# Reordering the first batch: value product square by square, keys tile by tile, the third context later

## The chip, the cores and the metric

The kernel runs on one core of a Trainium2 chip. The metric is the device time of one execution in microseconds (us), median of several runs. A core has TensorE (PE, matrix products), VectorE (DVE), ScalarE (ACT), GpSimd (POOL) and a queue of transfers that SyncE (SP) issues. Each works through its own list of instructions in order and waits on semaphores for the others.

## The reference, cut to what matters

Sixteen batches of `x`, each 512 rows by 512 columns in float32, pass through two layers:

```
x = x + xattn(layernorm(x), ctx, lens)
x = x + ffn(layernorm(x))

xattn:  h = rmsnorm(embeds) @ W_in.T + b_in
        u = rmsnorm(ctx)[..., :512] * gain          # input of a scan
        s = scan over the rows of ctx:  s[i] = a * s[i-1] + u[i]
        out = s[plug(row)] + h                      # rows of s picked by index
ffn:    xr = mu_r*y + (1-mu_r)*y_previous_row       # xk likewise
        r = sigmoid(xr @ W_r.T)
        k = square(relu(xk @ W_k.T))
        out = r * (k @ W_v.T)
```

`a` is so small that four shifted additions (by 8, 4, 2, 1 rows) of the first 128 rows give the scan. With these inputs no batch picks a row of `s` beyond the first 128, so the branches called `far` do nothing.

## The kernel before

A float32 product is made of three matmuls on a high part and a low part: high by high, high by low, low by high. `product` (L561 to L563) issues them. ACT makes the high part by a copy, DVE the low part by a subtraction (`low`, L1003). Every [512 x 512] product is 4 output tiles by 4 terms by 3 matmuls of 128x512, 48 in all. A batch has four such products and one turn by 16 transposes (`turn`, L697).

The work is a pipeline over batches, and its order is written out by hand for each engine, in an `iteration(b)` of each. While batch b is in the feed-forward layer, `nxt = b+1` is in the projection and its layer norm, and `new = b+2` is loaded and scanned. The stretch in question is `iteration(0)`: b is batch 0, nxt batch 1, new batch 2. Batches 0 and 1 have orders of their own (`is_first`), since the weights are still being split there.

On TensorE, iteration 0 runs `gate_product(0)`, `first_key_product(0)`, the value products of the four row tiles, and `turn(1)`. Iteration 1 follows with `project(2)`, `gate_product(1)`, `key_product(1)` and so on. What each waits for:

- `first_key_product` goes over pairs of output tiles (0, 1) and (2, 3), and within a pair over the four terms c. When a tile m is complete, `k_done` lets ACT make square m (`squares`: relu, square, high part), and then DVE its low part (`ka_low`, written to `xr_lo`).
- `value_product(b, t, first, last)` adds the terms m of row tile t, and at t = 0 waits for the low part of each square m.
- `turn(1)` needs `norm_b(1)` of DVE (L1211). That waits for a reciprocal root of POOL, `root_b` (L473).
- `project(2)` needs both halves of `x_lo(2)` of DVE (the low part of the turned x), which follow `x_hi(2)` of ACT.
- `gate_product(1)` needs the low parts of the mixed rows one by one. DVE's `mixing(1, ...)` makes these, at the head of its iteration 1: combine (L1136), high part on ACT, low part on DVE. Its tile 0 takes the terms c = 0 to 3 as they come.

The scan of batch 2 is spread over DVE's list. `squares_c` (ACT) sums the squares of the context, `stats_c` (DVE) scales the sum, `root_c` (POOL, L478) takes the root, `scan_input` (DVE, L1060) makes `u`. Then come four steps. Before each `scan_step`, SP shifts the last result down by two transfers into `above` (`shift_scan`, L366 and L367); they are issued when the step before is done. `add_bias` ends the scan, SP stores it, and POOL adds the picked rows to x by indirect transfers.

POOL's order in an iteration is `root_c(new)`, `root_b(nxt)`, `root_a(new)`, `add_patches(new)`. SP's is load x and turned x of `new`, the shifts and the store of the scan, then the four stores of b. `far_over` frees the context buffer for the next load.

Of the kernel before, what the change touches and what calls it, by code (L numbers as in the profile page):

```python
# [48 lines left out]
def reached(eng, semaphore, batch, per_batch, done):  # L49

    value = batch.number() * per_batch + done
    if isinstance(value, int) and value <= 0:
        return
    eng.wait_ge(semaphore, value)
# [35 lines left out]
def build(nc, x, x_turned, ctx, patch_lens, w_in, b_in, columns, g_init, w_r, w_k, w_v, out):  # L90

    B, S, D = x.shape
    DG = ctx.shape[2]
    C = D // P
    T = S // P
# [11 lines left out]
    with ExitStack() as stack:  # L107
# [135 lines left out]
        def tile(t):  # L243
            return slice(t * P, (t + 1) * P)

        def is_first(b, n=0):
            return b.fixed and b.number() == n
# [11 lines left out]
        def is_last(b):  # L259
            return b.fixed and b.number() == LAST  # L260
# [297 lines left out]
        def _(pe):  # L558
            def product(where, lhs_hi, lhs_lo, rhs_hi, rhs_lo, start, stop):

                nc.tensor.matmul(where, lhs_hi, rhs_hi, start=start, stop=False)  # L561
                nc.tensor.matmul(where, lhs_hi, rhs_lo, start=False, stop=False)  # L562
                return nc.tensor.matmul(where, lhs_lo, rhs_hi, start=False, stop=stop)  # L563
# [25 lines left out]
            def far(b):  # L589

                n = far_count(pe, b)
                with pe.If(n > 0):
                    earlier = far_earlier(pe, b)
                    for c in range(1, T):
                        done = earlier * (T - 1) + c
                        if c > 1:
                            pe.wait_ge(far_copied, done - 1)
                        else:
                            if b.fixed and b.number() < 2:
                                reached(pe, s_copied, b, 1, 1)  # L600
                            pe.wait_ge(far_u_lo, earlier * T + 1)

                        product(scan_bank(b)[:, :], decay_hi[:, 1, :], decay_lo[:, 1, :], u_hi[:, :], u_lo[:, :],
                                True, False).then_inc(far_carried, 1)
                        pe.wait_ge(far_u_lo, earlier * T + c + 1)
                        product(scan_bank(b)[:, :], decay_hi[:, 0, :], decay_lo[:, 0, :], u_hi[:, :], u_lo[:, :],
                                False, True).then_inc(far_s, 1)

                    pe.wait_ge(far_copied, earlier * (T - 1) + T - 1)
                    hold(pe, pe_passed)  # L610
# [22 lines left out]
            def first_key_product(b):  # L633


                for pair in ((0, 1), (2, 3)):
                    for c in range(C):
                        pe.wait_ge(w_lo_ready[WK], c + 1)
                        reached(pe, mix_lo_ready, b, 2 * C, C + c + 1)
                        for m in pair:  # L640
                            if c == 0:
                                reached(pe, x2_ready, b.plus(1), T, m + 1)
                            last = product(bank[m][:, :], wt_hi[WK][:, c, tile(m)], wt_lo[WK][:, c, tile(m)],
                                           xk_hi[:, c, :], xk_lo[:, c, :], c == 0, c == C - 1)
                            if c == C - 1:
                                last.then_inc(k_done, 1)

            def key_product(b):

# [51 lines left out]
            def iteration(b):  # L701
                nxt, new = b.plus(1), b.plus(2)
                if is_first(nxt):
                    first_steps(new)
                    return
                if nxt.exists(B) and not is_first(nxt, 1):
                    project(nxt)
                if b.exists(B) and not is_last(b):
                    gate_product(b)
                    key_product(b)  # L710
                    if is_last(nxt):
                        turn(nxt)

                    value_product(b, 0, 0, C - 1)
                    value_product(b, 1, 0, C - 1)
                    value_product(b, 0, C - 1, C)
                    value_product(b, 1, C - 1, C)
                if is_last(b):
                    key_product(b)
                    gate_product(b)  # L720
                    for t in range(T - 1):
                        value_product(b, t, 0, C)
                    value_halves(b, T - 1)
                if new.exists(B):
                    far(new)
                if b.exists(B) and not is_last(b):
                    for t in range(2, T):
                        value_product(b, t, 0, C)
                if nxt.exists(B) and not is_last(nxt):
                    turn(nxt)  # L730
# [80 lines left out]
        def _(act):  # L811
# [34 lines left out]
            def squares_c(b):  # L846
                reached(act, ctx_loaded, b, 16, 16)
                reached(act, v_c_done, b.plus(-1), 1, 1)
                nc.scalar.activation(ctx_squared[:, :], ctx_of(b)[:, :], ACT.Square, accum_out=v_c[:, 0:1]).then_inc(ms_c_done, 1)
# [74 lines left out]
            def iteration(b):  # L924
                nxt, new = b.plus(1), b.plus(2)
                if b.exists(B):
                    if is_last(b):
                        mix_hi(b, C, 2 * C)
                        squares(b)
                        gates(b)  # L930
                    elif is_first(b):
                        mix_hi(b, 0, C)
                        weight_hi(WK)
                        mix_hi(b, C, C + 2)
                        gates(b)
                        mix_hi(b, C + 2, C + 3)
                        weight_hi(WV, 0, 2)
                        mix_hi(b, C + 3, 2 * C)
                        squares_c(new)
                        weight_hi(WV, 2, C)  # L940
                    else:
                        mix_hi(b, 0, 2 * C)
                        if new.exists(B):
                            squares_c(new)
                        gates(b)
                if is_first(b):
                    squares(b)
                if is_first(b, 1):
                    squares(b)
                if new.exists(B) and not is_first(new, 1):  # L950
                    x_hi(new, 0)
                    x_hi(new, 1)
                if b.exists(B) and not is_last(b) and not is_first(b) and not is_first(b, 1):
                    squares(b)
                if is_last(nxt):
                    turned_out(nxt)
                    mix_hi(nxt, 0, C)
                if is_first(nxt):
                    x_hi(new, 1)

                    reached(act, far_over, nxt, 1, 1)
                    squares_c(new)
                    weight_hi(WR, 0, 1)
                    turned_out(nxt)
                if nxt.exists(B) and not is_last(nxt) and not is_first(nxt):
                    turned_out(nxt)
# [23 lines left out]
        def _(dve):  # L990
# [244 lines left out]
            def iteration(b):  # L1235
# [55 lines left out]
                if is_first(b):  # L1291
                    add_x(nxt, 2)
                    add_x(nxt, 3)
                    stats_c(new)
                    weight_lo(WV, 2, C)
                    scan_input(new)
                    ka_low(b, 0)
                    clear_head(new)
                    statistics_b(nxt, 0)
                    statistics_b(nxt, 1)  # L1300
                    ka_low(b, 1)
                    stats_b(nxt, 2)
                    scan_step(new, 0)
                    ka_low(b, 2)
                    ka_low(b, 3)
                    norm_b(nxt)
                    scan_step(new, 1)
                    stats_a(new)
                    scan_step(new, 2)
                    gating(b, 0)  # L1310
                    gating(b, 1)
                    x_lo(new, 0)
                    x_lo(new, 1)
                    scan_step(new, 3)
                    add_bias(new)
                    far(new)
                    dve.sem_inc(far_over, 1)
                    add_out(b, 0)
                    add_out(b, 1)
                    gating(b, 2)  # L1320
                    gating(b, 3)
                    add_out(b, 2)
                    add_out(b, 3)
                    return
                if nxt.exists(B):
                    add_x(nxt, 0)
# [191 lines left out]
```

## Time and profile before

| what | value |
|---|---|
| median of 3 runs | 763.27 us (761.37 to 763.87) |
| the profiled execution, its time | 761.57 us |
| its span | 760.0 us |
| PE busy | 745.4 us (98%) |
| DVE busy | 586.7 us (77%) |
| ACT busy | 405.5 us (53%) |
| POOL busy | 171.7 us (23%) |
| mean granted clock of TensorE | 0.991 |

The profile is of one execution, and all times in it count from the start of its span. A row of the timeline is: start, duration, engine, line, operation, output <- inputs, shape, number of instructions merged, and in brackets the idle time ahead of it with what ended it. A PE busy for 98% of the span leaves some 15 us in which it waited, nearly all of it in the first 80 us.

### The profile page before, as it was taken

How to read it: one execution, taken by the hardware profiler on the slowest of the kernel's cores; microseconds unless marked ns; L12 is line 12 of the kernel's file. 1: busy time of each engine (PE TensorE's matmuls, PEld its weight loads, DVE VectorE, ACT ScalarE, POOL GpSimd, SP SyncE). 2: the span in 40 equal slices, each digit the busy share in tenths (PEclk: the TensorE clock that was granted, in tenths of full speed). 3: DMA queues.
4: the chain of work that ended last, by engine and by line, in shares of the span. 5: the costliest groups of instructions: out<-in, count | busy, mean ns of one | idle time of the engine just before them, and what ended most of it. 6: DMA issues, size and time to landing. Idle time of an engine off the chain costs nothing.

```text
span 760.0 us, 11067 instructions
## 1 busy us (share of the span) xinstructions
PE 745.4 (98%) x3432; PEld 616.0 (81%) x3433; DVE 586.7 (77%) x1063; ACT 405.5 (53%) x666; POOL 171.7 (23%) x163
## 2 busy tenths in 40 slices
PE   7988999999999999999999999999999999999998
PEld 5866788888888888888888888888888888888887
DVE  7888996887869778696876879778696977867462
ACT  4177354754545556453754545465364655544860
POOL 6441230313131031312113131121312113130000
PEclk9999999999999999999999999999999999999999
DMA  8667371726446272633716355281634627240011
GB/s 308 172 194 187 117 200 56 206 98 154 138 112 180 69 185 104 159 135 93 205 54 162 129 137 166 79 222 56 153 125 109 193 67 192 96 125 14 1 56 56
DMA packets 51453, 100.02 MB, mean 132 GB/s; under 512 B 5134, under 2 KB 5390, under 8 KB 51388
## 3 DMA queue, kind: packets, MB, share of 16 engines
q1 hardware_dynamic: 41900, 82.46, 31.6%
q0 software_dynamic: 9216, 16.78, 13.4%
q8 instruction: 14, 0.23, 0.1%
q14 instruction: 35, 0.29, 0.1%
q10 hardware_dynamic: 288, 0.27, 0.1%
HBM read 64.26 MB, written 21.76 MB: 113 GB/s over the span
## 4 chain that ended last, share of the span: by engine, by line
PE 92%; DMA 4%; POOL 1%; DVE 1%; issue 1%; ACT 0%; SPq 0%; DVEq 0%; POOLq 0%
PE bank L561 29%; PE bank L562 29%; PE bank L563 29%; PE bank L697 3%; POOL ring L505 1%; DMA ring<-s_rows,patch_now 1%; DMA xt<-in_L_ffn_W_r 1%; PE bank L791 1%; DMA ring<-s_rows,patch_of 1%; DMA above<-u 1%; DMA s_rows<-scanned 1%; PE bank L770 0%; DMA ctx_rows<-in_ctx 0%; DMA lens<-in_mask_BxS_if 0%; POOL rs_a L459 0%
## 5 line engine op out<-in xcount | busy, mean ns | idle before, releaser
L505 POOL DMA_INDIRECT ring<-s_rows,patch_now x60 | 99.9, 1665 | 228.8 <-DMA s_rows<-scanned 198.1
L1136 DVE SCALAR_TENSOR_TENSOR scratch<-turned,cols,scratch 128x512 f32<-128x512 f32 x128 | 94.4, 748 | 32.0 <-ACT scratch L862 21.9
L1003 DVE TENSOR_TENSOR xr_lo<-scratch,xr_hi 128x512 fp32r<-128x512 f32 x124 | 85.1, 688 | 39.8 <-ACT xr_hi L813 38.9
L813 ACT ACTIVATE turned<-bank 128x512 f32<-128x512 f32 x64 | 33.1, 604 | 131.1 <-PE bank L697 131.1
L561 PE MATMUL bank<-wi_hi,xt_hi 128*128 128x512 f32 x256 | 101.9, 398 | 0.0
L561 PE MATMUL bank<-xk_hi,wk_hi 128*128 128x512 f32 x256 | 100.0, 391 | 1.0 <-DVE xk_lo L1003 0.6
L563 PE MATMUL bank<-wi_hi,xt_lo 128*128 128x512 f32 x256 | 100.6, 393 | 0.0
L562 PE MATMUL bank<-wi_lo,xt_hi 128*128 128x512 f32 x256 | 100.5, 393 | 0.0
L561 PE MATMUL bank<-wr_hi,xr_hi 128*128 128x512 f32 x256 | 100.1, 391 | 0.0
L562 PE MATMUL bank<-wr_lo,xr_hi 128*128 128x512 f32 x256 | 100.0, 391 | 0.0
L563 PE MATMUL bank<-wr_hi,xr_lo 128*128 128x512 f32 x256 | 99.8, 390 | 0.0
L563 PE MATMUL bank<-xk_hi,wk_lo 128*128 128x512 f32 x256 | 99.6, 389 | 0.0
L562 PE MATMUL bank<-xk_lo,wk_hi 128*128 128x512 f32 x256 | 99.6, 389 | 0.0
L561 PE MATMUL bank<-wv_hi,xr_hi 128*128 128x512 f32 x240 | 94.4, 394 | 2.6 <-DVE xr_lo L1003 2.6
L562 PE MATMUL bank<-wv_lo,xr_hi 128*128 128x512 f32 x240 | 94.0, 392 | 0.0
L563 PE MATMUL bank<-wv_hi,xr_lo 128*128 128x512 f32 x240 | 93.9, 391 | 0.0
L862 ACT ACTIVATE scratch<-turned,cols 128x512 f32<-128x512 f32 x128 | 89.5, 710 | 0.5
L813 ACT ACTIVATE xr_hi<-scratch 128x512 fp32r<-128x512 f32 x124 | 77.9, 628 | 21.1 <-DVE scratch L1136 19.1
L1217 DVE TENSOR_TENSOR gate<-bank,gate 128x512 f32<-128x512 f32 x63 | 42.6, 689 | 54.2 <-PE bank L563 54.2
L898 ACT ACTIVATE gate<-bank 128x512 f32<-128x512 f32 x64 | 37.2, 593 | 68.9 <-PE bank L563 68.8
L813 ACT ACTIVATE xk_hi<-scratch 128x512 fp32r<-128x512 f32 x64 | 40.5, 632 | 45.5 <-DVE scratch L1136 44.8
L909 ACT ACTIVATE scratch<-bank 128x512 f32<-128x512 f32 x64 | 38.2, 597 | 41.1 <-PE bank L563 37.7
(148 smaller groups left out, 1267.1 us busy)
## 6 DMA issues: line engine op xcount, KB each, us to landing
ring<-in_x SPq DMA_DIRECT2D x16, 1024.0 KB, 5.2
out<-gate SPq DMA_DIRECT2D x63, 256.0 KB, 2.1
xt<-in_x_turned SPq DMA_DIRECT2D x14, 1024.0 KB, 7.2
above<-scanned SPq DMA_DIRECT2D x42, 224.0 KB, 2.7
ctx_rows<-in_ctx SPq DMA_DIRECT2D x15, 512.0 KB, 5.9
s_rows<-scanned SPq DMA_DIRECT2D x15, 256.0 KB, 2.5
above<-u SPq DMA_DIRECT2D x14, 224.0 KB, 2.7
gate<-in_L_xattn_W_in SPq DMA_DIRECT2D x4, 256.0 KB, 3.5
```

The costliest lines, as they stand in the source:

```text
L505: pool.indirect_dma_start(ring[b.slot][:, t, :], None, s_rows[:, :], bass.IndirectOffsetOnAxis(ap=rows, axis=0), compute_op=ALU.add).then_ ...
L561: nc.tensor.matmul(where, lhs_hi, rhs_hi, start=start, stop=False)
L562: nc.tensor.matmul(where, lhs_hi, rhs_lo, start=False, stop=False)
L563: return nc.tensor.matmul(where, lhs_lo, rhs_hi, start=False, stop=stop)
L697: last = nc.tensor.transpose(first_bank(b, t)[:, tile(c)], normed[:, t, c * P:(c + 1) * P], ident[:, :])
L813: return nc.scalar.activation(to, of, ACT.Copy)
L862: nc.scalar.activation(scratch[:, i % 2, :], turned[:, c, 0:S], ACT.Copy, scale=cols[:, 3 + which, c:c + 1]).then_inc(carried, 1)
L898: nc.scalar.activation(gate[:, t, :], bank[4 + t][:, :], ACT.Sigmoid).then_inc(gate_ready, 1)
L909: nc.scalar.activation(scratch[:, m % 2, :], bank[m][:, :], ACT.Relu).then_inc(relu_ready, 1)
L1003: return nc.vector.tensor_tensor(to, whole, high, ALU.subtract)
L1136: nc.vector.scalar_tensor_tensor(scratch[:, 2 + i % 2, :], turned[:, c, 1:S + 1], cols[:, 1 + which, c:c + 1], scratch[:, i % 2, :], ALU.m ...
L1217: nc.vector.tensor_tensor(gate[:, t, :], bank[4 + t][:, :], gate[:, t, :], ALU.mult).then_inc(gated, 1)
```

## The change

There are four edits, all in the first batches' own orders.

1. TensorE, keys: tiles 0 and 1 stay interleaved; tiles 2 and 3 now come one after the other, so tile 2 is complete 12 matmuls before tile 3.
2. TensorE, values: for batch 0, the four row tiles take term 0, then all take term 1, and so on, where before tiles 0 and 1 took terms 0 to 2, then term 3, and tiles 2 and 3 followed whole.
3. ACT: `squares_c(2)` moves from ahead of the squares of batch 0 (and of the last two weight copies) to behind them.
4. DVE: `stats_c(2)` and `scan_input(2)` move behind the low parts of all four squares, and `scan_input` behind `norm_b(1)` too; the statistics of batch 1 come earlier; `x_lo(2)` comes after scan step 0 and no longer after step 2; `far(2)` and the release of the context buffer go to the end.

A wait of `far` on TensorE for the last `gated` is added inside a branch that is not entered here.

```diff
@@ TensorE, far
+                            if is_first(b, 2):
+                                reached(pe, gated, Batch(0, 0), T, T)
@@ TensorE, first_key_product
-                for pair in ((0, 1), (2, 3)):
-                    for c in range(C):
+                order = [(m, c) for c in range(C) for m in (0, 1)] + [(m, c) for m in (2, 3) for c in range(C)]
+                for m, c in order:
+                    if m == 0:
                         pe.wait_ge(w_lo_ready[WK], c + 1)
                         reached(pe, mix_lo_ready, b, 2 * C, C + c + 1)
-                        for m in pair:
...
@@ TensorE, iteration
+                    if is_first(b):
+                        for m in range(C):
+                            for t in range(T):
+                                value_product(b, t, m, m + 1)
+                    else:
...
-                if b.exists(B) and not is_last(b):
+                if b.exists(B) and not is_last(b) and not is_first(b):
                     for t in range(2, T):
                         value_product(b, t, 0, C)
@@ ScalarE, iteration
                         mix_hi(b, C + 3, 2 * C)
-                        squares_c(new)
                         weight_hi(WV, 2, C)
...
                 if is_first(b):
                     squares(b)
+                    squares_c(new)
@@ VectorE, iteration, is_first(b)
                     add_x(nxt, 2)
                     add_x(nxt, 3)
-                    stats_c(new)
                     weight_lo(WV, 2, C)
-                    scan_input(new)
+                    statistics_b(nxt, 0)
                     ka_low(b, 0)
-                    clear_head(new)
-                    statistics_b(nxt, 0)
                     statistics_b(nxt, 1)
                     ka_low(b, 1)
                     stats_b(nxt, 2)
+                    ka_low(b, 2)
+                    clear_head(new)
+                    ka_low(b, 3)
+                    stats_c(new)
+                    norm_b(nxt)
+                    scan_input(new)
                     scan_step(new, 0)
-                    ka_low(b, 2)
-                    ka_low(b, 3)
-                    norm_b(nxt)
+                    x_lo(new, 0)
+                    x_lo(new, 1)
                     scan_step(new, 1)
                     stats_a(new)
                     scan_step(new, 2)
                     gating(b, 0)
                     gating(b, 1)
-                    x_lo(new, 0)
-                    x_lo(new, 1)
                     scan_step(new, 3)
                     add_bias(new)
-                    far(new)
-                    dve.sem_inc(far_over, 1)
                     add_out(b, 0)
                     add_out(b, 1)
                     gating(b, 2)
                     gating(b, 3)
                     add_out(b, 2)
                     add_out(b, 3)
+                    far(new)
+                    dve.sem_inc(far_over, 1)
```

## Rows read from the trace of the kernel before

**Rows 1.** The page's first part: busy time, share of the span, instructions.

```profile
PE 745.4 (98%) x3432; PEld 616.0 (81%) x3433; DVE 586.7 (77%) x1063; ACT 405.5 (53%) x666; POOL 171.7 (23%) x163
```

**Rows 2.** Busy time by stretch, core 0, with TensorE's granted clock (PEclk).

```profile
core 0: us, PE busy (x) PEld busy (x) DVE busy (x) ACT busy (x) POOL busy (x), PEclk, DMA share, GB/s
76.80:80.10 3.30, 3.22 (x8) 2.55 (x9) 3.30 (x8) 1.05 (x2) 0.30 (x1) 0.52 0.25 77
120.00:160.00 40.00, 40.00 (x187) 33.35 (x186) 32.74 (x60) 22.88 (x37) 10.55 (x8) 1.00 0.49 145
```

**Rows 3.** Waits: total us, times, longest; TensorE for squares' low parts.

```profile
PE bank L561 <- DVE xr_lo L1003: 2.6, 2, 2.4
```

**Rows 4.** Timeline of TensorE, end of the keys to the next gate product.

```profile
66.86 0.47 PE L561 MATMUL bank<-xk_hi,wk_hi 128*128 128x512 f32 x1 [0.23 <-DVE ring L1170]
...
72.44 0.39 PE L561 MATMUL bank<-wv_hi,xr_hi 128*128 128x512 f32 x1
...
73.56 0.50 PE L561 MATMUL bank<-wv_hi,xr_hi 128*128 128x512 f32 x1 [0.28 <-DVE xr_lo L1003]
...
76.88 0.79 PE L561 MATMUL bank<-wv_hi,xr_hi 128*128 128x512 f32 x1 [2.35 <-DVE xr_lo L1003]
...
88.13 1.91 PE L697 MATMUL bank<-ident,normed 128*128 128x128 f32 x16
89.80 0.48 PE L561 MATMUL bank<-wi_hi,xt_hi 128*128 128x512 f32 x1
...
102.85 0.39 PE L561 MATMUL bank<-wr_hi,xr_hi 128*128 128x512 f32 x1
```

**Rows 5.** Timeline of ScalarE, the third context's squares and square 0.

```profile
66.52 1.06 ACT L849 ACTIVATE ctx_squared<-ctx_rows 128x1024 bf16<-128x1024 f32 x1 [2.39 <-DMA ctx_rows<-in_ctx]
...
68.62 0.58 ACT L909 ACTIVATE scratch<-bank 128x512 f32<-128x512 f32 x1
...
69.89 0.63 ACT L813 ACTIVATE xr_hi<-scratch 128x512 fp32r<-128x512 f32 x1
```

**Rows 6.** Timeline of VectorE, iteration 0 to the first mixed rows.

```profile
65.97 1.40 DVE L1170 SCALAR_TENSOR_TENSOR ring<-bank,rs_a,ring 128x512 f32<-128x512 f32 x2
...
69.43 0.75 DVE L1060 SCALAR_TENSOR_TENSOR u<-ctx_rows,rs_c,g_ctx 128x512 f32<-128x512 f32 x1
...
73.43 1.26 DVE L1175 BATCH_NORM_STATS2 bn_b<-ring 128x6 f32<-128x512 f32 x2
...
75.53 0.69 DVE L1081 SCALAR_TENSOR_TENSOR scanned<-above,u 128x512 f32<-128x512 f32 x1
...
77.34 1.91 DVE L1211 TENSOR_SCALAR normed<-ring,mv_b,rs_b 128x512 f32<-128x512 f32 x4
79.17 0.68 DVE L1081 SCALAR_TENSOR_TENSOR scanned<-above,scanned 128x512 f32<-128x512 f32 x1
...
82.91 0.69 DVE L1081 SCALAR_TENSOR_TENSOR scanned<-above,scanned 128x512 f32<-128x512 f32 x1
...
86.99 0.68 DVE L1081 SCALAR_TENSOR_TENSOR scanned<-above,scanned 128x512 f32<-128x512 f32 x1
...
88.97 1.29 DVE L1028 TENSOR_TENSOR gate<-gate,ring 128x512 f32<-128x512 f32 x2 [0.57 <-issue]
...
92.58 1.41 DVE L1136 SCALAR_TENSOR_TENSOR scratch<-turned,cols,scratch 128x512 f32<-128x512 f32 x2
...
98.19 0.69 DVE L1003 TENSOR_TENSOR xr_lo<-scratch,xr_hi 128x512 fp32r<-128x512 f32 x1
```

**Rows 7.** Timeline of VectorE, batch 4's scan: a step waiting for its shift.

```profile
158.77 0.71 DVE L1081 SCALAR_TENSOR_TENSOR scanned<-above,u 128x512 f32<-128x512 f32 x1 [0.21 <-issue]
...
162.44 0.69 DVE L1081 SCALAR_TENSOR_TENSOR scanned<-above,scanned 128x512 f32<-128x512 f32 x1 [1.13 <-DMA above<-scanned]
```

**Rows 8.** Timeline of GpSimd: the roots, each released by VectorE.

```profile
67.94 0.57 POOL L478 TENSOR_TENSOR rs_c<-v_c,half 128x1 f32<-128x1 f32 x1 [8.80 <-DVE v_c L1050]
75.58 1.52 POOL L473 TENSOR_TENSOR rs_b<-v_b,half 128x4 f32<-128x4 f32 x1 [7.08 <-DVE v_b L1185]
...
203.78 1.01 POOL L459 TENSOR_TENSOR rs_a<-v_a,half 128x4 f32<-128x4 f32 x1 [2.33 <-DVE v_a L1043]
```

More of the change, by code:

```diff
@@ L633, in first_key_product @@
             def first_key_product(b):
-                for pair in ((0, 1), (2, 3)):
-                    for c in range(C):
+                order = [(m, c) for c in range(C) for m in (0, 1)] + [(m, c) for m in (2, 3) for c in range(C)]
+                for m, c in order:
+                    if m == 0:
                         pe.wait_ge(w_lo_ready[WK], c + 1)
                         reached(pe, mix_lo_ready, b, 2 * C, C + c + 1)
-                        for m in pair:
[L641 to L646, printed above, removed]
+                    if c == 0:
+                        reached(pe, x2_ready, b.plus(1), T, m + 1)
+                    last = product(bank[m][:, :], wt_hi[WK][:, c, tile(m)], wt_lo[WK][:, c, tile(m)],
+                                   xk_hi[:, c, :], xk_lo[:, c, :], c == 0, c == C - 1)
+                    if c == C - 1:
+                        last.then_inc(k_done, 1)
             def key_product(b):
@@ L712, in iteration @@
                         turn(nxt)
[L714 to L717, printed above, removed]
+                    if is_first(b):
[3 more added lines that the diff above has]
+                    else:
+                        value_product(b, 0, 0, C - 1)
+                        value_product(b, 1, 0, C - 1)
+                        value_product(b, 0, C - 1, C)
+                        value_product(b, 1, C - 1, C)
                 if is_last(b):
```

## The prediction, on record before the run

> **What bounds the kernel now.** I read the page's first part first: TensorE is busy for 98% of the span [rows 1]. The busy times by stretch then say where the other 2% cannot be. From 120 to 160 us PE is busy for all 40.00 us at a granted clock of 1.00 [rows 2], so later batches lose nothing and can only be delayed. The waits show what is left: low parts of squares held PE twice, for 2.6 us [rows 3]. The timeline of PE places both in batch 0's value product, 0.28 us ahead of 73.56 and 2.35 us ahead of 76.88 [rows 4]. After the second the granted clock is 0.52 until 80.10 [rows 2]. That is the lower of its two levels, 1.2 GHz for 2.4, and it came after a stretch in which PE was mostly idle.
>
> **PE's pace.** From 89.80 to 102.85 PE starts 57 matmuls (48 of `project(2)`, 9 of tile 0 of `gate_product(1)`), 0.229 us each [rows 4]. The value product's 48 would need 11.0 us, and took 88.13 - 72.44 = 15.7 [rows 4]. So edits 1 to 3 can give back at most 4.7 us.
>
> **Squares after the change.** ACT no longer sits 2.39 us waiting for the third context [rows 5]; squares 0 and 1 follow their keys. Square 2: its keys start at 66.86 and end 12 matmuls later, near 69.9 with the last one's own length. Square 3: its keys still end near 72.6, as the last matmul starts one pace ahead of 72.44 and lasts 0.39 [rows 4]. A square is ready 69.89 + 0.63 - 68.62 = 1.90 us after its relu starts [rows 5], so square 3's high part is there at 74.5. DVE makes the low part by 75.3. The new order asks for term 3 only 36 matmuls after 72.44, at 80.7. PE therefore runs through: values end at 83.4. The turn takes 89.80 - 88.13 = 1.67 us [rows 4] and ends at 85.1. Cost of the value stage: minus 4.7 us. The new key order issues the same matmuls behind the same waits, so I charge it nothing; if tile 3's `add_x` were late it would wait less than before.
>
> **What DVE then does.** This is where I choose to carry the sum, since DVE's list holds all else. I lay it out in its new order. A tensor_tensor costs 0.60 us (six between 88.97 and 92.58), four norms 79.17 - 77.34 = 1.83, the end of `stats_b` 75.53 - 73.43 = 2.10, a scan step 0.6, `x_lo` twice 82.91 to 86.99 less a step and two gatings, 2.27 [rows 6].
>
> - `add_x` ends its turn at 67.3 [rows 6]; two weight lows to 68.5; then statistic, `ka_low(0)`, statistic, `ka_low(1)` to 70.9; `stats_b` to 73.0; `ka_low(2)` to 73.6; the small memset hides in the wait for square 3; `ka_low(3)` 74.6 to 75.2.
> - `squares_c` starts on ACT when square 3 is made, 74.5, and takes 1.06 us and a short read of its sum [rows 5], I take 1.15. So `stats_c` runs at 75.65. POOL's list has `root_c` ahead of `root_b`, and `norm_b(1)` is behind `root_b`: the root that `norm_b` wants is now queued behind the moved one. `root_c` takes 0.57; the four-column root 1.52 or, in another place, 1.01 [rows 8]; I take 1.2 as DVE stands still meanwhile. Norms start at 77.7, end at 79.5. The turn wants them at 83.4, so this costs PE nothing.
> - `u` is ready at 80.3, 10.1 us later than now (69.43 + 0.75 [rows 6]). Then nothing lies between it and scan step 0. The shift's round trip is seen where a step waited: 158.77 + 0.71 to 162.44 is 2.96 us [rows 7]. I take 2.9; the upper end is 75.53 - 70.18 = 5.35 [rows 6], with the big loads in the queues, the lower end is 0 if it hid. Step 0 at 83.2.
> - `x_lo` twice is queued behind step 0: 83.8 to 86.1. PE, free at 85.1, starts `project(2)` at 86.2, against 89.80 now. It is 3.6 us ahead at this point, and of the 4.7 us 1.1 is gone.
> - Step 1 waits for its shift until 83.9 + 2.9 = 86.8. Step 2 follows 82.91 - 79.17 = 3.74 later [rows 6], 90.5. Two gatings to 92.35. Step 3 waits for its shift until 91.2 + 2.9 = 94.1. Step and bias to 95.4, six output and gating instructions of 0.60 to 99.0, and 0.57 for `far`'s register part [rows 6]: `mixing(1)` starts at 99.6.
>
> **Where that lands.** `mixing(1)` starts at 92.58 now; its fourth low part ends at 98.19 + 0.69 = 98.9, and PE used it at 102.85 [rows 4, 6]. So DVE has a lead of 4.0 us, and it becomes 7.0 us later. As a balance: new waits of 0.6 (square 3), 0.4 (`squares_c`), 1.9 (two roots), 2.9, 0.7 and 1.8 (three shifts) are 8.3; some 1.1 of old waits disappear. The fourth low part ends at 105.9. PE would have reached it at 86.2 + 57 x 0.229 = 99.3. It stands idle near 97.2 for the first low part and then takes three matmuls at a time. From tile 0's last term PE runs on, 105.95 against 102.85: plus 3.1 us. Whatever PE gained before is consumed by this wait, so the end is set by DVE: 7.0 - 4.0 = 3.0 and 0.1 of release.
>
> **The clock.** After the idle ahead of 76.88 eight matmuls ran at the low level, which cost 8 x 0.2 = 1.6 us [rows 2, 4]. The idle at 97 to 102 is longer. Most of the low stretch should fall under the one-by-one low parts, where PE waits anyway. Between 0 and 1.6 I take 0.5.
>
> **Afterwards.** The scan's store, the indirect adds and `add_x(2)` shift by the same 7 us as DVE; the key product of batch 1 shifts by 3.1 only. Its first tile needs `add_x(2, 0)`, now used over ten us after it is made, so this stays covered. DVE is busy 77% of the span [rows 1] and has waits in later batches, so it catches up during batch 1. SP: `far_over` comes later and delays the load of context 3, which ACT needs after the mixing that is late itself: nothing. The out stores wait for the same DVE rows: nothing.
>
> **Sum.** 761.57 + 3.1 + 0.5 = 765.2 for an execution like the profiled one, whose span is 760.0. Its time lies 1.7 us below the median 763.27, so against the median it is 763.27 + 3.6 = 766.9.
>
> **A page against the row.** The shift's round trip is 2.96 us in the row [rows 7]. The Trainium skill (DMA: Bandwidth & Descriptors, Anatomy of one DMA) gives a fit of about 2.0 us fixed plus bytes over 436 GB/s, taken on the GpSimd path; an estimate from it for 224 KB is 2.5 us. By that page the three waits would be shorter by some 1.2 us together and the result about plus 2.4. The row decides, since it includes SP's two issues.
>
> **The rivals.**
>
> - *The shifts come back under other work* (the other side). If each round trip cost DVE nothing, 5.4 of the 8.3 us of waits vanish, `mixing(1)` is late by 1.6, inside its lead of 4.0, and PE keeps what it gained at `project(2)`: minus 3.6, or minus 4.7 if `x_lo` is not late either, 757 to 760 in the profile, about 759.4 on the median. It decides from the point where `mixing(1)` is less than about 4.0 us late. For it: step 0 to 3 were never held by a shift in iteration 0 now. Against it: there 5 to 7 us of work lay between steps, now 0 after `u`. Chance 0.07.
> - *The delay is about as large as the lead*, from shorter shifts and a `root_b` of 1.01 us: `mixing(1)` late by 4 to 6, change between -2.3 and +2.3, centre 764.5. Chance 0.18.
> - *DVE does not catch up*, so that key or value product of batch 1 stalls too, or the low clock holds PE through the one-by-one terms: another 2 to 5 us, 769 to 772 on the median. Against it: the idle DVE has while waiting for squares in steady batches. Chance 0.13.
> - *The turn is held by late norms*: ready at 79.5 for 83.4; it would take 4 us more of roots. Within the cases above.
>
> **How the numbers follow.** My forecast has 0.62. Its own ends: a shift trip of 2.7 to 3.3, a root of 1.0 to 1.5, clock 0 to 1.6, give plus 2.3 to plus 5.8. With the rivals the range for 8 in 10 is 763.6 to 769.8. A change of 0.3% (2.3 us) is about what a measurement can tell from none. Slower by more: 0.62 + 0.13 = 0.75; within: 0.18; faster: 0.07.
>
> **What would show it.** In the profile after: no wait for `xr_lo` in batch 0's value product and 11.0 us for it; `squares_c` right behind square 3; scan step 0 released by a transfer, not by DVE's own list; PE waiting 1.1 us for `xt_lo` ahead of `project(2)`; and a wait of 4 to 5 us ahead of `gate_product(1)` with three smaller ones, released by `xr_lo`. If that last wait is under 1 us, the prediction is wrong.

## The result

The changed kernel takes 765.79 us (median of 5 runs, 765.62 to 767.77), the kernel before 763.27 us in the same set. The ratio is 1.0051, with a 95% interval of 1.0030 to 1.0072. So it is slower by about half a per cent, 2.5 us on the medians. The profiled execution took 765.79 us, its span is 764.2 us against 760.0.

The waits of TensorE in the profile after (total us, times, longest):

```profile
PE bank L561 <- DVE xr_lo L1010: 4.9, 1, 4.9
...
PE bank L561 <- DVE u_lo L1010: 3.1, 1, 3.1
PE bank L561 <- DVE xt_lo L1010: 0.8, 1, 0.8
```

`xr_lo` is a name for two things: low parts of the squares in the value product, and low parts of the mixed rows in the gate product. Before, two waits of 2.6 us together stood for it [rows 3]; now there is one of 4.9. The wait for `u_lo` belongs to the start-up and is in the kernel before too, with 3.3 us. The timeline of TensorE after says which it is:

```profile
72.01 0.39 PE L561 MATMUL bank<-wv_hi,xr_hi 128*128 128x512 f32 x1
...
82.90 1.91 PE L699 MATMUL bank<-ident,normed 128*128 128x128 f32 x16
85.59 0.47 PE L561 MATMUL bank<-wi_hi,xt_hi 128*128 128x512 f32 x1 [0.78 <-DVE xt_lo L1010]
...
101.58 0.77 PE L561 MATMUL bank<-wr_hi,xr_hi 128*128 128x512 f32 x1 [4.86 <-DVE xr_lo L1010]
...
105.72 0.73 PE L561 MATMUL bank<-wr_hi,xr_hi 128*128 128x512 f32 x1
```

The value product runs from 72.01 to 82.90 without a wait, where it took 15.7 us [rows 4]. `project(2)` begins 2.69 us behind the start of the turn, not 1.67. Then TensorE has nothing for 4.86 us ahead of `gate_product(1)`. The last term of its tile 0 starts at 105.72, against 102.85 [rows 4].

ScalarE after makes the squares behind their keys, and the context's squares last:

```profile
65.64 0.60 ACT L916 ACTIVATE scratch<-bank 128x512 f32<-128x512 f32 x1 [0.80 <-PE bank L563]
...
72.21 0.60 ACT L916 ACTIVATE scratch<-bank 128x512 f32<-128x512 f32 x1 [0.75 <-PE bank L563]
...
74.05 1.04 ACT L856 ACTIVATE ctx_squared<-ctx_rows 128x1024 bf16<-128x1024 f32 x1
```

The timeline of VectorE after shows what that does to the scan:

```profile
74.17 0.69 DVE L1010 TENSOR_TENSOR xr_lo<-scratch,xr_hi 128x512 fp32r<-128x512 f32 x1 [0.48 <-ACT xr_hi L820]
75.21 0.15 DVE L1057 TENSOR_SCALAR v_c<-v_c 128x1 f32<-128x1 f32 x1 [0.35 <-ACT ctx_squared L856]
77.05 1.92 DVE L1218 TENSOR_SCALAR normed<-ring,mv_b,rs_b 128x512 f32<-128x512 f32 x4 [1.69 <-POOL rs_b L473]
78.88 0.75 DVE L1067 SCALAR_TENSOR_TENSOR u<-ctx_rows,rs_c,g_ctx 128x512 f32<-128x512 f32 x1
82.48 0.69 DVE L1088 SCALAR_TENSOR_TENSOR scanned<-above,u 128x512 f32<-128x512 f32 x1 [2.85 <-DMA above<-u]
83.09 2.35 DVE L1010 TENSOR_TENSOR xt_lo<-xt,xt_hi 128x1024 fp32r<-128x1024 f32 x2
86.02 0.69 DVE L1088 SCALAR_TENSOR_TENSOR scanned<-above,scanned 128x512 f32<-128x512 f32 x1 [0.57 <-DMA above<-scanned]
...
90.50 0.69 DVE L1088 SCALAR_TENSOR_TENSOR scanned<-above,scanned 128x512 f32<-128x512 f32 x1 [0.67 <-DMA above<-scanned]
...
94.05 0.69 DVE L1088 SCALAR_TENSOR_TENSOR scanned<-above,scanned 128x512 f32<-128x512 f32 x1 [1.66 <-DMA above<-scanned]
...
99.30 1.41 DVE L1143 SCALAR_TENSOR_TENSOR scratch<-turned,cols,scratch 128x512 f32<-128x512 f32 x2 [0.23 <-issue]
...
107.59 0.75 DVE L1177 SCALAR_TENSOR_TENSOR ring<-bank,rs_a,ring 128x512 f32<-128x512 f32 x1 [1.99 <-issue]
```

and that of GpSimd the two roots in a row:

```profile
75.46 0.57 POOL L478 TENSOR_TENSOR rs_c<-v_c,half 128x1 f32<-128x1 f32 x1 [16.64 <-DVE v_c L1057]
76.00 1.01 POOL L473 TENSOR_TENSOR rs_b<-v_b,half 128x4 f32<-128x4 f32 x1
```

Up to 99.30, the brackets of the seven rows that wait for another engine or a transfer add up to 8.3 us, where the same stretch before had 1.1 us of such waits (0.32, 0.37 and 0.38). The first mixed rows of batch 1 start at 99.30, against 92.58 [rows 6]. The last row is `add_x(2, 0)`, the first use of the picked rows of batch 2; it began at 98.80 before, without a wait.

The clock, by stretches of the profile after (the last three columns: granted clock, transfer share, GB/s):

```profile
72.01:82.90 10.89, 10.89 (x49) 8.96 (x48) 5.44 (x15) 4.80 (x7) 1.56 (x2) 1.00 0.11 39
...
101.50:107.50 6.00, 5.92 (x13) 3.98 (x14) 4.03 (x6) 4.58 (x8) 4.32 (x3) 0.50 0.97 206
```

The value product now runs at full clock. The low level, 1.2 GHz, has moved to the gate product of batch 1, from 101.5 to 107.5, behind the 4.86 us of idle time.

**Landmarks.** One profiled execution differs from the next in the start-up: the first key product of batch 0 begins anywhere between 59.0 and 62.6 us in the profiles of this study, and all of the edits lie behind that point. The rest, from `turn(2)` to the end, takes 626.5 to 628.8 us in them, and both profiles of the changed kernel (626.6 and 627.3) lie near the kernel before (626.5), so nothing of the change shows there. Spans therefore cannot be compared to a microsecond. I take the stages between TensorE's landmarks instead, each the difference of two start times in the timeline, in us:

```
                        keys   values  turn   project  gate    key    value   keys(0)
                        (0)    (0)     (1)    (2)      (1)     (1)    (1)     to turn(2)
before                  13.01  15.69   1.67   11.01    10.88   10.88  10.89   74.03
changed                 12.77  10.89   2.69   15.99    13.96   10.88  11.21   78.39
changed_again           12.20  10.89   2.69   16.12    13.05   10.88  11.92   77.75
values_old_order        12.20  10.92   2.65   15.68    13.06   10.88  12.10   77.49
root_b_first            12.20  10.88   1.67   15.82    13.75   10.88  11.10   76.30
waits_filled            13.22  10.89   1.66   13.18    13.70   10.88  12.44   75.97
tensor_orders_alone     12.92  10.89   3.68   10.97    10.88   10.88  10.89   71.11
values_alone            13.02  10.88   3.86   11.00    10.88   10.88  10.88   71.40
tensor_orders_early_x   12.83  10.89   1.67   10.97    11.33   10.88  10.89   69.46
early_x_alone           12.26  16.13   1.66   11.02    10.88   10.88  10.88   73.71
lead_5_fillers          12.25  13.31   1.67   10.98    11.67   10.88  10.88   71.64
lead_12_fillers         12.84  15.70   1.66   12.18    13.05   10.88  10.89   77.20
```

A stage runs from its first instruction to the first of the next, so a wait counts to the stage ahead of it. The changed kernel: minus 4.8 for the values, plus 1.0, plus 5.0, plus 3.1, plus 0.3, and minus 0.2 in the keys, which vary from 12.2 to 13.2 in these profiles, make plus 4.4.

### The profile page after: what moved, and what is told of

It reads as the page before. It is cut to its first block, busy times and chain, and to the rows that moved or that the text cites. A ratio compares the mean times of both kernels' runs of the same rounds, so it can differ in the third digit from the quotient of the medians.

```text
span 764.2 us, 11063 instructions
## 1 busy us (share of the span) xinstructions
PE 747.0 (98%) x3432; PEld 616.1 (81%) x3433; DVE 586.7 (77%) x1063; ACT 405.5 (53%) x666; POOL 170.2 (22%) x163
## 4 chain that ended last, share of the span: by engine, by line
PE 89%; DMA 4%; issue 3%; DVE 2%; POOL 2%; ACT 1%; SPq 0%; DVEq 0%; POOLq 0%
PE bank L561 28%; PE bank L563 28%; PE bank L562 28%; PE bank L699 3%; POOL ring L505 1%; DMA above<-scanned 1%; PE bank L798 1%; DMA xt<-in_L_ffn_W_r 1%; DMA ring<-s_rows,patch_of 1%; DMA s_rows<-scanned 1%; PE bank L777 0%; DVE scanned L1088 0%; DMA above<-u 0%; DMA lens<-in_mask_BxS_if 0%; ACT turned L820 0%
## 5 line engine op out<-in xcount | busy, mean ns | idle before, releaser
L561 PE MATMUL bank<-wr_hi,xr_hi 128*128 128x512 f32 x256 | 101.7, 397 | 4.9 <-DVE xr_lo L1010 4.9
L561 PEld LDWEIGHTS bank<-wr_hi,xr_hi 128*128 128x128 f32 x256 | 48.9, 191 | 16.8 <-issue 5.5
```

## The experiments

Theory A is that of the prediction: VectorE's new waits make the first mixed rows late, TensorE pays ahead of and within `gate_product(1)`, and its own new orders gain 4.7 us that are used up there. Theory B is stated with each run. Ratios are to the kernel before, with 95% intervals.

### The changed kernel again (changed_again)

> The changed kernel as it is, as the measure for the other runs of this call. Theory A (VectorE's new waits put the first mixed rows of batch 1 late and TensorE pays for it ahead of gate_product(1)): 4.2 us over the kernel before in the profiled span, ratio 1.003 to 1.007, mixing(1) at about 99.3 us. Theory B (the time is lost elsewhere, by the low clock or by noise): the wait ahead of gate_product(1) varies and the loss with it.

Ratio 1.0058 (1.0040 to 1.0075). Mixing starts at 99.23, TensorE waits 5.00 us. The medians are 767.68 and 763.26 us, plus 4.4. Up to the gate product the picture repeats. Then the low clock ends some two us earlier, and the gate stage is 13.05 instead of 13.96; but the value stage of batch 1 is 11.92 instead of 11.21. Counted from the first matmul of the values, `turn(2)` starts at 65.55 us here and at 65.62 in the first profile, against 61.02 before. So the 0.9 us that the clock took in one execution was no loss at the end: something else holds TensorE later in batch 1 (see Afterwards, below).

### Values in the old order (values_old_order)

```diff
-                    if is_first(b):
-                        for m in range(C):
-                            for t in range(T):
-                                value_product(b, t, m, m + 1)
-                    else:
-                        value_product(b, 0, 0, C - 1)
...
+                    value_product(b, 0, 0, C - 1)
+                    value_product(b, 1, 0, C - 1)
+                    value_product(b, 0, C - 1, C)
+                    value_product(b, 1, C - 1, C)
```

> The changed kernel with the value product of batch 0 in the old order (tiles 0 and 1 take terms 0 to 2, then term 3, tiles 2 and 3 whole). Theory A: the low parts of the squares are ready at 69.4, 70.6, 73.2 and 74.9 us in the changed kernel, the old order asks for them at 72.1, 72.8, 73.5 and 76.2, so there is no wait either and nothing changes against the changed kernel, within 0.3 us of its span. Theory B (the square by square order is what removed the wait for xr_lo): the 2.4 us wait in the value product is back; TensorE reaches project(2) later, and the end is the same or, with a shorter idle time ahead of gate_product(1), up to 1 us earlier.

Ratio 1.0057 (1.0035 to 1.0078); the value stage takes 10.92 us in the old order too. The raw span, 766.4 us, is not within the 0.3 us expected; from the first keys to `turn(2)` it is, 77.49 against 77.75. In the changed kernel the square by square order is worth nothing that shows: the other edits had already removed the wait. Which of them did it no run separates. Edits 1 and 3 bring the squares earlier, but edit 4 has a part too. In the kernel before, ScalarE had the high part of square 2 at 74.15, and VectorE, busy with statistics and scan step 0, made the low part only from 76.14 on. ScalarE's row before, and VectorE's:

```profile
73.52 0.63 ACT L813 ACTIVATE xr_hi<-scratch 128x512 fp32r<-128x512 f32 x1
```

```profile
76.14 1.29 DVE L1003 TENSOR_TENSOR xr_lo<-scratch,xr_hi 128x512 fp32r<-128x512 f32 x2
```

### The norms' root first (root_b_first)

```diff
-                if new.exists(B) and not is_first(nxt):
+                if new.exists(B) and not is_first(nxt) and not is_first(b):
                     root_c(new)
                 if nxt.exists(B):
                     root_b(nxt)
+                if is_first(b):
+                    root_c(new)
```

> The changed kernel with GpSimd's root_b(1) ahead of root_c(2) in iteration 0. Theory A (each us of VectorE's waits after the squares is a us of the end): the norms start at 75.4 instead of 77.05 us, u at 77.2 instead of 78.9, the scan steps, the mixed rows and the end come 1.7 us earlier: span about 762.5 against 764.2. Theory B (VectorE's waits are cover and the clock or the transfers set the end): span within 0.5 us of the changed kernel's.

Ratio 1.0034 (1.0020 to 1.0049), 1.0058 without this edit; the medians differ by 0.9 us, and from the first keys to turn(2) it is 76.30 against 77.75 us. Its timeline of VectorE shows the wait gone:

```profile
77.98 0.15 DVE L1059 TENSOR_SCALAR v_c<-v_c 128x1 f32<-128x1 f32 x1 [0.35 <-ACT ctx_squared L858]
78.06 1.91 DVE L1220 TENSOR_SCALAR normed<-ring,mv_b,rs_b 128x512 f32<-128x512 f32 x4
...
92.07 0.69 DVE L1090 SCALAR_TENSOR_TENSOR scanned<-above,scanned 128x512 f32<-128x512 f32 x1 [1.25 <-DMA above<-scanned]
```

Counted from the first matmul of the values, the norms start at 3.28 us against 5.04 in `changed_again`, so 1.76 us of wait are gone, and mixing starts at 26.08 against 27.42, 1.34 us earlier. The rest went to a longer wait for the third shift, 1.25 us for 0.80. Theory B said within 0.5 us of the changed kernel's span; the raw span, 766.0 us, is even longer, but the keys start 3.0 us later in that profile, ahead of every edit. The landmarks decide for A, with a size a little under it: counted from the first matmul of the values, `turn(2)` starts at 64.10 us, 1.5 earlier than in both profiles of the changed kernel. The medians go the same way, though their intervals overlap.

### VectorE's waits filled (waits_filled)

```diff
                     scan_input(new)
-                    scan_step(new, 0)
                     x_lo(new, 0)
                     x_lo(new, 1)
-                    scan_step(new, 1)
+                    scan_step(new, 0)
                     stats_a(new)
-                    scan_step(new, 2)
+                    scan_step(new, 1)
                     gating(b, 0)
                     gating(b, 1)
-                    scan_step(new, 3)
-                    add_bias(new)
                     add_out(b, 0)
                     add_out(b, 1)
+                    scan_step(new, 2)
                     gating(b, 2)
                     gating(b, 3)
                     add_out(b, 2)
                     add_out(b, 3)
+                    scan_step(new, 3)
+                    add_bias(new)
                     far(new)
```

> The changed kernel with VectorE's waits for the shifted rows filled: x_lo(2) ahead of scan step 0, the statistics of x ahead of step 1, gating and output of tiles 0 and 1 ahead of step 2, of tiles 2 and 3 ahead of step 3. Theory A: mixing(1) starts at about 95.1 instead of 99.3 us, the fourth low part is there at 101.4, so the end is 4.2 us earlier than the changed kernel's and 0 to 1.1 us before the kernel before (ratio 0.998 to 1.001), project(2) starts at 84.6 right behind the turn. Theory B: filling VectorE's waits gives less than 1 us.

Ratio 1.0025 (1.0009 to 1.0040), 2.5 us under the changed kernel's median, not the 4.2 expected. The part that I worked out came nearly as said: counted from the first matmul of the values, mixing starts at 23.45 us against 27.42 in `changed_again`, 4.0 us earlier. `project(2)` follows the turn (1.66), and the wait for the first mixed rows fell from 5.00 to 2.04 us, in the timeline of TensorE:

```profile
100.11 0.47 PE L561 MATMUL bank<-wr_hi,xr_hi 128*128 128x512 f32 x1 [2.04 <-DVE xr_lo L1010]
...
101.41 0.50 PE L561 MATMUL bank<-wr_hi,xr_hi 128*128 128x512 f32 x1 [0.36 <-DVE xr_lo L1010]
...
102.80 0.80 PE L561 MATMUL bank<-wr_hi,xr_hi 128*128 128x512 f32 x1 [0.37 <-DVE xr_lo L1010]
```

The projection's stage is 2.9 us shorter and the turn's 1.0. But the gate stage is 0.65 us longer than in `changed_again`; from 102.80 to 104.00 the granted clock is 0.50. And the value stage of batch 1 is 0.5 us longer. What holds it shows in two rows of VectorE's timeline:

```profile
106.80 0.75 DVE L1177 SCALAR_TENSOR_TENSOR ring<-bank,rs_a,ring 128x512 f32<-128x512 f32 x1 [2.67 <-issue]
108.21 0.75 DVE L1177 SCALAR_TENSOR_TENSOR ring<-bank,rs_a,ring 128x512 f32<-128x512 f32 x1 [0.66 <-DMA ring<-s_rows,patch_now]
```

and in one of ScalarE's:

```profile
123.87 0.60 ACT L916 ACTIVATE scratch<-bank 128x512 f32<-128x512 f32 x1 [2.49 <-DVE xr_lo L1010]
```

The scan's end moved less than the mixing, so the picked rows of batch 2 are added late, and VectorE stands at `add_x(2, 0)`. It is then late with the low parts of batch 1's squares, ScalarE waits for them, and the value stage of batch 1 takes 12.44 us for the 10.89 of the kernel before. The changed kernel loses 1.0 us of its own there (11.92). The release of 106.80 is called "issue" in the row. That it is the first indirect transfer follows from the transfer's own time. The view of transfers gives, from issue to landing in us, for the first one in `waits_filled` and in `changed_again`:

```profile
ring<-s_rows,patch_now POOLq DMA_INDIRECT x1, 5.8
```

```profile
ring<-s_rows,patch_now POOLq DMA_INDIRECT x1, 9.0
```

GpSimd issues them at 100.90 and 98.21, so they land at 106.7 and 107.2, and `add_x(2, 0)` starts at 106.80 and 107.33.

### TensorE's two orders alone (tensor_orders_alone)

The kernel before with edits 1 and 2, the hunks of `first_key_product` and of TensorE's `iteration` as in the diff of the change, and nothing else.

> The kernel before with the two new orders of TensorE alone (keys tile by tile in the second pair, values square by square); ScalarE and VectorE as before. Theory A: squares 2 and 3 are there at 76.8 and 77.4 us, asked for at 77.9 and 80.6, so the value product has no long wait and ends at 83.4; project(2) then waits for xt_lo until 87.1 (now 89.8); mixing(1) stays at 92.6, inside its lead. Minus 2.7 us, with a low clock behind the wait of 2 us minus 1.1: ratio 0.9965 to 0.9985. Theory B (TensorE's new orders gain nothing that lasts, something further down takes it back as in the changed kernel): ratio 1.000.

Ratio 0.9979 (0.9964 to 0.9995). The value stage takes 10.89 us, the stage of the turn 3.68 with a wait of 1.77 us for `xt_lo`, and the gate stage is untouched at 10.88. From the first keys to turn(2) it is 2.9 us shorter, for the 2.7 expected, and 1.6 us on the medians. The low clock expected behind the wait did not come: the projection takes 10.97 us.

### The value order alone (values_alone)

The same without the new key order, so that only the hunk with `value_product(b, t, m, m + 1)` and its condition remain.

> The kernel before with the square by square value product alone; keys stay in two interleaved pairs, ScalarE and VectorE as before. Theory A: ScalarE begins square 0 at 68.6 us, later than its keys, and makes one each 1.8 us, so the time at which tile 2's keys are complete does not matter; the same as with both orders of TensorE, ratio about 0.998, value product 10.9 us. Theory B (the tile by tile keys are needed for it): a wait for xr_lo stays in the value product, 1 to 2 us, ratio 0.999 to 1.001.

Ratio 0.9973 (0.9954 to 0.9993), value stage 10.88 us. With ScalarE and VectorE as before, the whole gain comes from edit 2, and edit 1 adds nothing.

### The low part of x earlier, alone and with TensorE's orders (early_x_alone, tensor_orders_early_x)

```diff
                     norm_b(nxt)
                     scan_step(new, 1)
-                    stats_a(new)
+                    x_lo(new, 0)
+                    x_lo(new, 1)
+                    gating(b, 0)
                     scan_step(new, 2)
-                    gating(b, 0)
-                    gating(b, 1)
-                    x_lo(new, 0)
-                    x_lo(new, 1)
+                    stats_a(new)
                     scan_step(new, 3)
+                    gating(b, 1)
```

This is on top of edits 1 and 2. Alone, on the kernel before, the run has the same moves, but with both gatings behind scan step 3.

> As the run with TensorE's orders alone, and on VectorE x_lo(2) moved up behind scan step 1, gating(0) ahead of step 2, the statistics of x behind it. No new wait of VectorE but 0.1 us. Theory A: project(2) starts right behind the turn at 85.1, mixing(1) at about 92.7; the fourth low part at 99.0 holds TensorE by some 0.8 us; minus 3.8 us against the kernel before, ratio 0.995. Theory B: ratio 1.000.

> The kernel before with x_lo(2) moved up behind scan step 1 on VectorE and TensorE as before. Theory A: project(2) follows the turn without a wait in the kernel before, so an earlier x_lo gives nothing by itself, and gating(0) later has cover: ratio 1.000, the values still take 15.7 us. Theory B (the gain of the run with both came from VectorE's order alone): ratio 0.996 or less.

Alone the ratio is 1.0000 (0.9984 to 1.0016). With TensorE's orders it is 0.9943 (0.9923 to 0.9963), 758.71 us against 763.04 of the kernel before in the same set. This is the fastest version of the study and beats both kernels: 4.3 us on the medians, 4.6 from the first keys to `turn(2)`, for the 3.8 expected. The turn's stage is 1.67 us. The gate stage is 0.45 us longer than before, where 0.8 was expected, and of waits for mixed rows the timeline shows one:

```profile
99.79 0.50 PE L561 MATMUL bank<-wr_hi,xr_hi 128*128 128x512 f32 x1 [0.15 <-DVE xr_lo L1008]
```

### VectorE's lead, measured by fillers (lead_5_fillers, lead_12_fillers)

```diff
                     add_out(b, 2)
                     add_out(b, 3)
+                    for i in range(5):            # 12 in the second run
+                        nc.vector.bn_stats(spare[:, 6 * i:6 * i + 6], bias[:, :])
                     return
```

> The kernel before with 5 added bn_stats on VectorE (of the bias, to a spare tile) between the last output of batch 0 and mixing(1), 3.0 us. Theory A (VectorE has a lead of 4.0 us at that place): ratio 1.000, no wait of TensorE ahead of gate_product(1). Theory B (no such lead): plus 3.0 us.

> The kernel before with 12 such fillers, 7.3 us. Theory A: 7.3 less the lead of 4.0 is 3.3 us, and about 1 us of low clock behind the idle time: plus 3.3 to 4.3 us, ratio 1.0043 to 1.0056, with the same picture ahead of gate_product(1) as in the changed kernel. Theory B (the loss in the changed kernel came from the scan's transfers, not from the late start of mixing(1)): plus 0 or plus 7.

Five fillers: ratio 0.9995 (0.9978 to 1.0012). Twelve: 1.0057 (1.0039 to 1.0074). So 3 us of added VectorE work cost nothing that the runs can tell, and 7.3 us cost, within the intervals, as much as the whole change does. The timeline of TensorE with twelve:

```profile
101.72 0.47 PE L562 MATMUL bank<-wr_hi,xr_hi 128*128 128x512 f32 x1 [1.04 <-DVE xr_lo L1004]
...
105.80 0.50 PE L562 MATMUL bank<-wr_hi,xr_hi 128*128 128x512 f32 x1 [0.43 <-DVE xr_lo L1004]
```

Counted from the first matmul of the values, mixing starts 7.13 us later than in the kernel before (27.27 for 20.14) and the last term of tile 0 3.21 us later (33.62 for 30.41), so the lead is 3.9 us. The stages projection and gate are 1.2 and 2.2 us longer, 3.3 in all. The low clock that was expected on top did not come: the granted clock is 1.00 from 101.7 to 106.0.

This run also divides the loss. Its mixing starts as late as in the changed kernel (27.27 us for 27.29 and 27.42), but its scan is in time, `add_x(2, 0)` does not wait, and the value stage of batch 1 keeps 10.89 us. `turn(2)` is 3.3 us late there and 4.6 and 4.5 in the changed kernel. So 3.3 us need no scan and no transfer, only a late start of `mixing(1)`; the other 1.2 or so go with the late scan.

With five fillers TensorE did have short waits for the gate terms, where none was expected, and its stage was 11.67 us for 10.88. In that execution the value stage had kept full clock, 13.31 us for 15.69, so TensorE came earlier and the lead was smaller.

## Why the prediction was right

**The sum and the range.** The forecast was 766.9 us (763.6 to 769.8), measured is 765.79. Against the kernel before that is plus 2.5 us on the medians and, in the second set, plus 4.4, where plus 3.6 was forecast; the profiled span gives plus 4.2. The mechanism came as told, late mixed rows that TensorE waits for, and it makes up 3.3 of the 4.5 us. That the sum fits so well is in part luck: the term for the clock stood in for a wait in batch 1 that was put at nothing. The forecast's own ends, added up, reach plus 6.2, not 5.8.

**TensorE's gain.** Said: minus 4.7 us, values in 11.0. Measured: minus 4.8, 10.89. The prediction credited edits 1 to 3 together. The experiments tell them apart in part: in the changed kernel edit 2 does nothing; on the kernel before it does everything.

**The roots.** Said: 1.9 us of wait for `norm_b`, since `root_b` stands behind `root_c`; measured 1.69, as the four-column root took 1.01 us, the lower of the two rows shown. Taking the order away gave back most of it.

**The shifts.** Said: waits of 2.9, 0.7 and 1.8 us; measured 2.85, 0.57 and 1.66, and 0.67 at step 2, where I expected none. This is also why the whole of VectorE's new waits came out at the 8.3 us forecast: the unexpected wait makes up for the others, each a little shorter. The estimate from the Trainium skill (DMA: Bandwidth & Descriptors, Anatomy of one DMA), a shift of 2.5 us, is for one transfer; the profile's view of transfers has 2.7 us from issue to landing for those of 224 KB, and the trip that the sum needs, from VectorE's result to its next step, is 2.85 (78.88 + 0.75 to 82.48). One reading of the rows was wrong: it is not 5 to 7 us of work that lay between the steps before. The steps are 3.6 to 4.1 us apart, so about 3.0 to 3.5 us of other work lay between them, and 5.35 us ahead of the first [rows 6]. A trip of 2.9 was only just covered.

**The lead.** Said: 4.0 us of lead, 7.0 of delay, plus 3.1 at the last term of tile 0. Measured: mixing 6.7 us later, TensorE 2.9 us later at that term; each is 0.2 more if the keys' earlier start by 0.2 is counted. The difference is the lead, 3.85 us. The fillers give 3.9.

**The clock.** Said: 0.5 us, between 0 and 1.6, most of the low stretch falling under the one-by-one terms. (The rows give 3.22 us for the eight slow matmuls, 1.4 us more than at full pace, not 1.6.) The low stretch lasted six us in one profile, to 107.5, and ran past tile 0's last term; it cost the gate stage another 1.0 us, and 0.1 in the other profile. The three smaller waits that I had named as a sign did not appear, since the slow matmuls filled the time; with twelve fillers, at full clock, they did. None of the 1.0 us is left at `turn(2)`, which starts at 65.62 and 65.55 us after the first matmul of the values.

**Afterwards.** Said: VectorE catches up during batch 1 at no cost. This is the step that failed, by about 1.2 us. The scan ends late, the first indirect transfer lands late, at 107.2 us in `changed_again`, and `add_x(2, 0)` waits 1.8 to 2.0 us for it. Behind it VectorE works nearly without a gap up to the squares of batch 1, and TensorE gets their low parts late. The rows of five kernels bear this out. `add_x(2, 0)` starts at 35.58, 35.52, 35.12, 34.04 and 32.42 us after the first matmul of the values in the changed kernel, `changed_again`, `values_old_order`, `root_b_first` and `waits_filled`, and `turn(2)` follows it by 30.0 to 30.3 us in all five, whatever the clock did between. In the kernel before it follows by 34.7 us, and in `lead_12_fillers` by 30.9. That the time is set there is my reading of these differences; no run moves `add_x(2, 0)` alone.

**What stays open.** Whether edit 3 alone, with VectorE's list before, would gain was not tried: `stats_c` would wait for ScalarE's squares. Which of edits 1, 3 and 4 removed the wait in the value product is not separated. Why the third shift takes longer, and why the first indirect transfer takes 9.0 us in one kernel and 5.8 in another, is not explained. Of the idle time of the kernel before, 3.1 of 14.6 us lie behind the first 80 us; none of the runs looks at them.

## What to carry to other kernels

A stall removed on the busiest engine is a gain only up to the lead of the engine that feeds its next stage; find that lead before moving work, by laying out the feeder's list with its waits, or with fillers as here. Work that another queue must return (a transfer, a root on another engine) wants other work behind it in the list: with no work left behind it, roots and shifts made 7.4 of VectorE's 8.3 us of waits here. A late engine can also cost twice: VectorE held TensorE at the mixed rows, and again two products later, because its own next input, at the end of the same scan, was late too. When two edits remove the same wait, the cheaper one alone is the version to keep: a few lines of TensorE's order gave 0.2 to 0.3%, and with `x_lo` moved up 0.6%, where the full change lost 0.5%.

## What the runs showed of the hardware

The low level of TensorE's clock does not last equally long from one execution to the next. Behind 76.88 it had passed after some eight matmuls [rows 2, 4]. In the changed kernel groups of three matmuls at low clock fill the time between two low parts, and it lasted from 101.5 to 107.5; in `changed_again`, with the same groups behind a wait of 5.00 us, it was 0.50 from 101.4 to 105.4 and 0.95 in the us behind that. After waits of 1.04 us and of 2.10 us (twelve fillers ahead of the gate product, five fillers in the values) it stayed at 1.00.

The third shift of the scan took longer than the others in all four profiles with this order of the scan (3.5 to 4.4 us). SP's timeline after shows one of its two issues taking twice its usual time:

```profile
83.20 0.54 SPq L366 DMA_DIRECT2D above<-scanned  x1
83.79 0.80 SPq L367 DMA_DIRECT2D above<-scanned  x1
86.74 0.52 SPq L366 DMA_DIRECT2D above<-scanned  x1
87.30 1.71 SPq L367 DMA_DIRECT2D above<-scanned  x1
```

From 86.02 + 0.69 to the next step at 90.50 it is 3.79 us, against 2.85 or 2.86 for the others. In `root_b_first` it is 4.4 with a usual issue time, so the long issue is not the whole of it.
